# Conditioned residual on one core: the input laid out in memory one load at a time

## The reference

```python
def reference(x, itok_B_1_198, L0_cond_weights):      # x 64x64x512, itok 64, weights 200x64x64
    w = weights[conditions]                           # one 64x64 matrix for each of 64 samples
    return x + jnp.einsum('bct,bcd->bdt', x, w)
```

## Time and profile before

| | |
|---|---|
| median of 3 runs | 46.12 us |
| lowest and highest | 46.06, 46.23 us |
| the profiled execution | 46.19 us, its span 44.9 us |
| HBM read, written | 9.44 MB, 8.39 MB |
| mean rate over the span | 397 GB/s |
| PE busy | 31.0 us (69%) |
| DVE, ACT busy | 15.1, 13.4 us |
| granted TensorE clock | full (2.4 GHz) in every slice |

### The profile page before, as it was taken

The page is one execution under the profiler, slowest core; times in us unless marked ns, Lnnn a source line. Parts: engine busy times, 40 slices in busy tenths (PEclk is TensorE's granted clock), DMA queues, the critical chain, the costliest instruction groups (busy, mean ns, idle before and its releaser), DMA issues.

```text
span 44.9 us, 331 instructions
## 1 busy us (share of the span) xinstructions
PE 31.0 (69%) x100; PEld 13.4 (30%) x100; DVE 15.1 (34%) x24; ACT 13.4 (30%) x16; POOL 1.6 (4%) x9
## 2 busy tenths in 40 slices
PE   0040000499999979999999699999999999920000
PEld 0040000433534144543453235344354453300000
DVE  1220000000009990758730490085086073063000
ACT  0894000000000064736710480085085071062000
POOL 4008100000000000000000000000000000000000
PEclk9999999999999999999999999999999999999999
DMA  0389999999999899999995989999998999999993
GB/s 0 81 314 431 424 431 431 424 431 431 416 438 519 372 467 467 467 467 467 438 467 248 438 380 424 409 453 438 424 424 372 409 424 424 431 424 394 402 438 153
DMA packets 1730, 17.83 MB, mean 397 GB/s; under 512 B 194, under 2 KB 194, under 8 KB 194
## 3 DMA queue, kind: packets, MB, share of 16 engines
q1 hardware_dynamic: 1584, 16.78, 89.2%
q0 software_dynamic: 144, 1.05, 5.5%
q10 hardware_dynamic: 2, 0.00, 0.0%
HBM read 9.44 MB, written 8.39 MB: 397 GB/s over the span
## 4 chain that ended last, share of the span: by engine, by line
DMA 50%; PE 31%; SPq 4%; DVE 3%; issue 1%; POOLq 0%
DMA x_sb<-x 50%; PE product L166 31%; SPq L94 4%; DVE y_sb L216 3%; POOLq L134 0%
## 5 line engine op out<-in xcount | busy, mean ns | idle before, releaser
L166 PE MATMUL product<-x_sb,w_diag 128*128 (+1 forms) x40 | 17.7, 597 | 0.4 <-POOLq L134 0.4
L216 DVE COPY y_sb<-product 128x1024 f32<-128x1024 f32 x8 | 9.8, 1224 | 12.9 <-PE product L166 10.5
L117 ACT COPY y_sb<-product 128x1024 f32<-128x1024 f32 x8 | 8.1, 1012 | 13.6 <-PE product L166 11.3
L146 PE MATMUL product<-x_sb 128*128 128x512 f32 x10 | 7.3, 907 | 5.4 <-DMA x_sb<-x 5.4
L166 PEld LDWEIGHTS product<-x_sb,w_diag 128*128 128x128 f32 x40 | 7.4, 190 | 10.5 <-issue 10.5
L158 PE MATMUL product<-x_sb,w_all 64*64 64x512 f32 x48 | 5.5, 601 | 0.3 <-DVE w_all L205 0.3
L146 PEld LDWEIGHTS product<-x_sb 128*128 128x128 f32 x10 | 2.9, 302 | 9.1 <-issue 9.1
L111 ACT COPY w_diag<-w_all 64x256 f32<-64x256 f32 x1 | 0.6, 642 | 12.3 <-DVE w_all L205 12.3
L202 DVE TENSOR_TENSOR gathered<-gathered,piece 128x64 f32<-128x64 f32 x1 | 0.3, 267 | 10.2 <-DMA gathered<-weights,table_row 10.2
L158 PEld LDWEIGHTS product<-x_sb,w_all 64*64 64x64 f32 x48 | 2.5, 200 | 3.3 <-issue 2.1
L205 DVE STREAM_TRANSPOSE w_all<-gathered 128x2048 f32<-128x2048 f32 x1 | 2.3, 2311 | 0.0
(11 more groups left out here) (9 smaller groups left out, 1.6 us busy)
## 6 DMA issues: line engine op xcount, KB each, us to landing
x_sb<-x SPq DMA_DIRECT2D x4, 1024.0 KB, 9.3
x_sb<-x SPq DMA_DIRECT2D x1, 4096.0 KB, 22.7
out<-y_sb SPq DMA_DIRECT2D x2, 2048.0 KB, 8.0
out<-y_sb SPq DMA_DIRECT2D x4, 1024.0 KB, 5.4
condition<-conditions ACTq DMA_DIRECT2D x1, 0.2 KB
gathered<-weights,table_row POOLq DMA_INDIRECT x1, 9.8
```

The lines of the kernel that those rows point to most:

```text
L117: nc.scalar.copy(y_sb[:, 4 * turn:4 * turn + 2, :], product[turn % SETS][0][:, :, :]).then_inc(moved_by_act, 1)
L146: nc.tensor.matmul(product[1][0][:, 0, :], x_sb[:, 0, 0:P], x_sb[:, 0, :], start=True, stop=True)
L166: product_of = nc.tensor.matmul(product[s][j][:, g, :], w_diag[:, s, 2 * j + g, :], x_pair(2 * j + g), start=True, stop=True)
L216: nc.vector.tensor_copy(y_sb[:, 4 * turn + 2:4 * turn + 4, :], product[turn % SETS][1][:, :, :]).then_inc(moved_by_dve, 1)
```

## The change

The host cuts `x` into five pieces, one for each load, and lays them behind one another. Within a piece, the 128 partitions' runs follow each other with no gap: partition 0's 8 KB of turn 0, then partition 1's, and so on; in the last piece 32 KB for each partition. The kernel's loads (now L96) take their source by a hand-written access pattern: offset `pairs.start * T * P`, a step of one run (8 KB, or 32 KB in the last load) from partition to partition. The destination in `x_sb`, the size of each load, the order of the loads and what waits for them stand as before. The result stays [128 partitions, 32 pairs, 512], with 64 KB from partition to partition, and the stores (now L104) are untouched. Neither the order nor the number of the instructions of any engine changes; lines after the edit move down by three.

```diff
-    P, PAIRS, T = x.shape
+    PAIRS, P, T = x.shape
...
             for first, last in LOADS:
                 pairs = pairs_of(first, last)
-                sp.dma_start(x_sb[:, pairs, :], x[:, pairs, :]).then_inc(x_loaded[first], 16)
+
+                run = (pairs.stop - pairs.start) * T
+                sp.dma_start(x_sb[:, pairs, :], bass.AP(x.tensor, pairs.start * T * P, [[run, P], [T, run // T], [1, T]])
+                             ).then_inc(x_loaded[first], 16)
...
     x_laid = np.asarray(x).reshape(B // PAIR, PAIR, C, T).transpose(1, 2, 0, 3).reshape(PAIR * C, B // PAIR, T)
 
+    pieces = [x_laid[:, first:first + n].reshape(-1) for first, n in ((0, 4), (4, 4), (8, 4), (12, 4), (16, B // PAIR - 16))]
+
...
-    arrays = {"x": np.ascontiguousarray(x_laid),
+    arrays = {"x": np.concatenate(pieces).reshape(B // PAIR, PAIR * C, T),
...
-    out = nc.dram_tensor("out", x_laid.shape, mybir.dt.float32, kind="ExternalOutput").ap()
+    out = nc.dram_tensor("out", (PAIR * D, B // PAIR, T), mybir.dt.float32, kind="ExternalOutput").ap()
```

## The result

The changed kernel takes 46.25 us (median of 22 runs, 46.02 to 46.44), the one before 46.06 us (22 runs, 45.87 to 46.34). The ratio is 1.0042 with a 95% interval of 1.003 to 1.0055: it is slower by 0.19 us, less than the 0.5% that I set as the least a measurement can tell, and yet clear of noise, since the interval does not hold 1. Twenty-two runs a side resolve more than I had allowed for.

A forecast was written before the change was run, and what follows sets the result against it. It took full DMA engines as the bound, with the store queue and PE's chain level at the end. All terms were zero: 46.19 + 0 = 46.19 us, less 0.07 to the median, 46.12, rounded 46.1; range 45.75 to 46.40.

The forecast's parts named there:

- no change that can be told: Whole kernel: likeliest case, time within 0.23 us of 46.12, that is 45.89 to 46.35 us; chance 0.70.
- What bounds the kernel: Whole kernel: DMA engines nearly full throughout; at the end the store queue and PE's chain level, neither with slack.
- The cap of 0.35 us from PE's gap: PE before turn 4: idle 0.35 us, so faster x shortens its chain by at most that, unless the gather comes earlier.
- The landing that I had named as the event that both depend on: Landing of the 4 MB load, 25.37 us: stores and PE's turn 4 both begin there; expected at 25.2 to 25.5.
- PE's gap before turn 4: Sign on PE between turns 3 and 4: if right, the gap stays between 0.1 and 0.5 us.
- the rate from 4.00 to 25.36 us: Sign in the stretch reading x and the gathered table: if right, it stays at 430 to 435 GB/s.
- Instructions and packets: All loads: issue costs nothing more, and 1584 packets stay with none longer or dropped; zero for both.
- The address step between packets: Reads of x: 64 KB step becomes 8 or 32 KB; between 0.14 us less and 0.92 us more, taken as zero.
- The start of the reads: From 1.75 to 4.00 us, 321 GB/s: 0.56 us of engine time missing; gain of 0 to 0.56, taken as zero.
- The rival of compact reads: Whole read stretch: engines crowding in one 1 MB block read slower, up to 0.92 us more, 47.04 us; chance 0.10.
- The rival of quick first reads: First reads: over 0.23 of the missing 0.56 us goes, giving 45.77 to 45.89 us; chance 0.12.
- The rival of the old step: All reads of x: rows 64 KB apart conflicted, compact ones are faster by 0.35 us or more, giving 45.77; chance 0.08.

The follow-up runs named there:

- e2: Kernel before, input tensor holding both layouts; only the load of turn 0 reads the compact one: 46.31 us, ratio 1.0046 to before.
- e3: Kernel before, input tensor holding both layouts; the load of turn 0 reads the old one, the other four the compact one: 45.99 us, ratio 0.9990.
- e1: Control: kernel before, input tensor holding both layouts, all five loads reading the old one (64 KB step): 46.06 us, ratio 1.0006.
- e7: Whole kernel with the old layout, except a 16 KB step between partitions in the load of turn 0: 46.42 us, ratio 1.0096 to before.
- e9: Only 16 separate 1 MB loads of x, each from idle engines, and one store; 16 KB step instead of 64 KB: 87.0 us.
- e12: Only 16 separate 1 MB loads of x, each from idle engines, and one store; 68 KB step instead of 64 KB: 79.3 us.
- e5: Kernel before without gather, products and all stores but one; 16 separate 1 MB loads, each after the last landed, 64 KB step: 78.8 us.
- e6: Only 16 separate 1 MB loads of x, each from idle engines, and one store; compact 8 KB step instead of 64 KB: 83.0 us.

## Why the prediction was right and wrong

**The time and the size.** 46.1 us was forecast with 45.75 to 46.4, and 46.25 was measured; "no change that can be told", 45.89 to 46.35, was the likeliest case, and 46.25 is within it. But I forecast a change of zero, and there is one of 0.19 us, to the slow side. The forecast time came near because the term that failed is small.

**What bounds the kernel** was half right. DMA engines that are full from about 3 us to the end: yes, and that is why 0.19 us at the start is still there at the end. That the chain over PE is level with the queue of stores was read from a sum within its rounding, and the queue is what sets the end: in the profiled execution of the changed kernel PE's chain was 0.32 us ahead of the one of before and the end did not move, and e2 and e3 issue their last store together and land it 0.3 us apart. The cap of 0.35 us from PE's gap therefore limits nothing here. The landing that I had named as the event that both depend on is that of the slowest engine, while the stores follow on each engine behind that engine's own loads. I said that I would be wrong in the reason if the landings moved by over 0.3 us without the time. Between the two profiled executions they did, 25.37 to 25.04 us; with e1 at 25.13 by the old layout, most of that is scatter from one execution to the next, so the landing was a bad sign to name. PE's gap before turn 4 (0.24 us) and the rate from 4.00 to 25.36 us (435 GB/s) came out as named.

**Instructions and packets** at zero: right, 1584 packets, the same sizes.

**The address step between packets**, bounded by 0.14 us less and 0.92 more and taken as zero: right for reads under way. e3 reads 7.3 of the 8.4 MB compactly and gives 0.9990. The ceiling of 435 GB/s that I took from the Trainium skill ("DMA: Bandwidth & Descriptors", section "Where 436 GB/s comes from") against a gain is in keeping with it: the window of 14 to 25 us gave 435 GB/s before, and no layout of these runs made the kernel faster by more than its interval. In the other executions that window reads 429 to 441 GB/s; the 441 of e7 lies above the ceiling, as a window that books packets by their start can.

**The start of the reads** is the step that failed. I priced it between 0 and 0.56 us of gain and took zero, and gave it no side for a loss, though the step itself said that 0.56 us of engine time is missing there, so that this is the one stretch of the reads that isn't limited by what the engines can pass. I took zero on the ground that the ramp is there for any address pattern and may be all of it. It measures 0.19 us of loss in the changed kernel, 0.25 in e2 beside e1, 0.26 for each separate load. The engines' time that was missing there was not all a ramp that any address pattern has: how early the engines begin and how long their first packets take depends on the addresses, so the term can go either way. What part of the 0.56 us is ramp stays open; no step that was tried made it smaller by more than the interval.

**The rival of compact reads** had the direction right and the place wrong: it put the loss on the whole read stretch, with 0.92 us, and it is confined to the first load, before 4 us. Its mechanism, engines that crowd in one block of 1 MB, is not shown, and e9 speaks against it as it stands. **The rival of quick first reads** fell with the sign of its term. **The rival of the old step** holding the reads back fell: with it, e3 would have been faster by 0.35 us, a ratio of 0.992, and its interval begins at 0.9968. The rule of the Trainium skill on large power-of-two pitches ("DMA: Bandwidth & Descriptors", section "Latency and other measured facts") names 512 KiB as its smallest pitch. No run here shows such a loss at 64 KB: with 4 KB of padding e12's two runs took 79.27 and 79.34 us, inside the 78.65 to 79.39 of e5. The advice beside that rule, tiles laid out contiguously, costs here: 0.26 us for each load that begins with idle engines (e6).

No version beat the kernel before. The nearest, e3, keeps the old step for the first load only and is the same within 0.2%.

## What to carry to other kernels

Where the DMA engines are full from the first load to the last store, the layout of the rest of the input made no difference that can be told (steps of 8 and 32 KB against 64), but the first load decides when the bytes begin to flow, and any delay there reaches the end undiminished. Give the load that starts from idle engines a wide step between partitions (64 KB here), and try more than one step, since the narrowest isn't the worst. Read a queue's lateness from the mean over its engines, not from one landing, and compare more than one execution before a shift of 0.3 us is put down to a change. And when a term is read from a stretch where the engines are slow for an unknown reason, bound it on both sides of zero.

## What the runs showed of the hardware that I had not expected

- A read of 1 MB that starts from idle takes from 4.5 us (64 KB between the rows of two partitions) to 5.0 us (16 KB) from issue to landing, with 4.8 at 8 KB (medians of 16 loads). In a running stream the median packet of 8 KB takes 309 ns whatever the step.
- A store of 1 MB from idle lands after 3.9 us, 0.6 us sooner than a load of the same size and step. Its first 16 packets take 311 to 321 ns in the records of e5; the first 16 to start of each load there take 307 to 1191 ns, 599 in the mean. The one store of these kernels has no slow start.
- Second reads of the same addresses are hardly quicker than first ones: a load of the second pass lasts 0.03 to 0.04 us less from its first packet to its last, in e5 and e6 alike, and the penalty of e6 was there in both passes.
